# Cross-attention maxima over all 13 tiles and three tiles earlier, shift rows as pieces copied by VectorE

## What is computed

```python
x = x + attend(adaln(x) @ Wq, adaln(ctx) @ Wkv) @ Wp          # "a0": cross-attention, context normalised
x = x + g * (attend(adaln(x) @ qkv) @ Wp)                     # "s1": self-attention
x = x + attend(ln(x) @ Wq, ctx @ Wkv) @ Wp                    # "c1": cross-attention, context raw
x = x + g * mlp(adaln(x))                                     # "m1"
x = x + g * (attend(adaln(x) @ qkv) @ Wp)                     # "s2"
x = x + attend(ln(x) @ Wq, ln(ctx) @ Wkv) @ Wp                # "c2": cross-attention, context normalised
x = x + g * mlp(adaln(x))                                     # "m2"
x = x + gate * experts(x, ctx)                                # "l3"
# attend: softmax(q k^T / sqrt(8)) v for each of the 16 heads
```

## Time and profile before

| what | value |
|---|---|
| time, median of 3 runs | 6270.36 us (6269.71 to 6271.52) |
| the profiled execution | 6276.06 us |
| its span in the profile | 6274.1 us |
| PE busy | 89% of the span |
| DVE busy | 66% |
| ACT busy | 69% |
| POOL busy | 16% |
| the chain that ended last | PE 63%, ACT 14%, DVE 10%, issue 4%, DMA 4%, POOL 3% |

### The profile page before, as it was taken

How to read it: one execution, slowest core, us unless ns; L and a number is a source line. 1 busy time by engine, 2 the same in 40 slices (tenths; PEclk the granted TensorE clock), 3 DMA queues, 4 the chain that set the end, 5 groups by cost and what they waited for, 6 DMA issues and landing times.

```text
span 6274.1 us, 225170 instructions
## 1 busy us (share of the span) xinstructions
PE 5577.9 (89%) x99544; PEld 3439.1 (55%) x99544; DVE 4131.0 (66%) x6523; ACT 4303.3 (69%) x8158; POOL 986.0 (16%) x1660
## 2 busy tenths in 40 slices
PE   5999999989878899999999878699999999998998
PEld 3555555555544455565556444355555555555665
DVE  5777777677555677777777355477777777754443
ACT  3777777777766688788887566467777777763333
POOL 3121121121111111111111011111221211200000
PEclk9999999999999999999999899899999999999999
DMA  2222212222112222222222011222222222211110
GB/s 89 83 67 65 85 57 75 73 61 79 42 57 66 86 74 69 75 86 77 77 67 76 11 59 57 70 61 85 69 63 85 67 65 85 65 52 32 46 57 26
DMA packets 230088, 414.17 MB, mean 66 GB/s; under 512 B 23904, under 2 KB 131472, under 8 KB 228624
## 3 DMA queue, kind: packets, MB, share of 16 engines
q1 hardware_dynamic: 229136, 400.04, 21.3%
HBM read 316.81 MB, written 83.14 MB: 64 GB/s over the span
## 4 chain that ended last, share of the span: by engine, by line
PE 63%; ACT 14%; DVE 10%; issue 4%; DMA 4%; POOL 3%; SPq 2%; DVEq 0%; ACTq 0%; POOLq 0%
PE bank L1087 23%; PE pair L1087 15%; PE bank L1195 12%; ACT P L1329 6%; DVE MX L1493 5%; ACT QP L1340 2%; DMA QP<-scr_q 2%; ACT REST L1300 2%; PE bank L700 2%; PE bank L691 1%; PE pair L627 1%; ACT KSF L1299 1%; PE pair L1182 1%; PE bank L1114 1%; DMA scr_ks<-KSF 1%
## 5 line engine op out<-in xcount | busy, mean ns | idle before, releaser
L1329 ACT ACTIVATE P<-bank 128x512 f32<-128x512 f32 (+1 forms) x5504 | 3185.4, 599 | 1080.0 <-PE bank L1087 1003.5
L1493 DVE TENSOR_REDUCE MX<-pair 128x2 f32<-128x802 f32 x3072 | 2927.6, 987 | 1088.5 <-PE pair L1087 1062.3
L1087 PE MATMUL bank<-QP,KP 128*32 128x256 bf16 (+2 forms) x40192 | 2167.9, 275 | 232.9 <-ACT P L1329 177.5
L1087 PE MATMUL pair<-KP,QP 96*32 96x401 bf16 (+2 forms) x25336 | 1801.3, 337 | 144.9 <-DMA QP<-scr_q 108.4
L1087 PEld LDWEIGHTS bank<-QP,KP 128*32 128x32 bf16 (+2 forms) x40192 | 1057.8, 96 | 1326.5 <-ACT P L1329 292.4
L1195 PE MATMUL bank<-P,VA 128*25 128x256 f32 (+1 forms) x22016 | 1739.1, 384 | 19.1 <-issue 18.6
L1087 PEld LDWEIGHTS pair<-KP,QP 96*32 96x32 bf16 (+1 forms) x25336 | 691.6, 97 | 347.3 <-DVE MX L1493 129.9
L1195 PEld LDWEIGHTS bank<-P,VA 128*25 128x25 f32 (+1 forms) x22016 | 625.7, 104 | 205.7 <-issue 76.9
L1497 DVE TENSOR_REDUCE MX<-pair 128x4 f32<-128x1024 f32 x256 | 311.3, 1222 | 332.3 <-PE pair L1087 331.5
L1618 POOL COPY VA<-VN 128x416 f32<-128x416 f32 (+1 forms) x320 | 140.7, 440 | 2360.8 <-PE bank L1195 2283.9
L1340 ACT CAST QP<-pair 2x512 bf16<-2x512 f32 x640 | 339.4, 576 | 144.1 <-PE pair L1182 132.2
(11 more groups left out here) (242 smaller groups left out, 4189.4 us busy)
## 6 DMA issues: line engine op xcount, KB each, us to landing
KP<-scr_k SPq DMA_DIRECT2D x768, 225.1 KB
QP<-scr_q SPq DMA_DIRECT2D x960, 48.0 KB
CN<-ctx_n SPq DMA_DIRECT2D x40, 768.0 KB
scr_k<-KSF SPq DMA_DIRECT2D x48, 600.8 KB, 3.2
scr_k<-KSF SPq DMA_DIRECT2D x48, 600.0 KB, 3.3
CT<-ctx_t SPq DMA_DIRECT2D x24, 800.5 KB, 4.5
KP<-scr_ks SPq DMA_DIRECT2D x128, 144.0 KB
scr_q<-QS SPq DMA_DIRECT2D x80, 192.0 KB, 2.1
```

What stands on the lines that cost most here:

```text
L1087: last = nc.tensor.matmul(out[c:c + m, :], lhsT[:, c:c + m], rhs, start=start, stop=stop)
L1329: nc.scalar.activation(P[v % 2][0:kt, half * 2 * N:(half + 1) * 2 * N], SC[half][0:kt, :], ACT.Exp, scale=SCALE).then_inc(sem("probs_full" ...
L1493: nc.vector.tensor_reduce(MX[:, r, c:c + 2], MP[j % 2][:, :].rearrange("p (t k) -> p t k", t=2)[:, :, 0:SPANS[0][1]], AX.X, ALU.max).then_ ...
```

## The change

In cross phases: `early` lays the 16 maximum steps evenly over 13 tiles, and `maxima` moves them three tiles ahead (`EARLY = 3`), so that steps 0 to 3 of the group after next run in tiles 10 to 12, and steps 4 to 15 of the next group in tiles 0 to 9. The shifts are then made in tile 9. The shift rows become two pieces of the MISC bank, "r" pieces in tiles 11 and 12 of each group; their products are made by PE and their copies to QP by DVE instead of ACT. The scores of tile 0 wait for those pieces' `misc_free`. In the shifts, the bf16 part is a second reduction of MX instead of a copy of NMF. The pieces of the next element get other slots. d and e are now made in strips of 32 columns. Self phases keep their order, but their last tile adds steps 0 to 3 for a cross phase that follows.

```diff
+EARLY = 3
-SHORT = ["mean", "var", "q", "k0", "k1", "k2", "k3", "y"]
+SHORT = ["mean", "var", "q", "k0", "k1", "k2", "k3", "d", "e", "y"]
...
+    def early(self, first, end):
+        return [j for j in range(self.nm) if first <= j * self.nt // self.nm < end]
+
     def prep_slots(self, host):
         if host.cross:
-            at = dict(mean=0, square=1, var=2, norm=2, q=6, v0=36)
+            at = dict(mean=0, square=1, var=2, norm=2, q=6, v0=34)
             if self.cross:
-                at.update({n: 5 + j * 8 // 13 for j, n in enumerate(STATS)})
-                at.update(ctx_scale=12, ctx_norm=12, t0=18, t1=19, k0=20, k1=22, t2=23, t3=24, k2=26, k3=28)
-                at.update(v1=38, v2=40, v3=45)
+                at.update({n: j * 8 // 13 for j, n in enumerate(STATS)})
+                at.update(ctx_scale=8, ctx_norm=8, t0=14, t1=15, k0=16, k1=18, t2=19, t3=20, k2=21, k3=23)
+                at.update(v1=36, v2=40, v3=42)
...
+            if ph.cross:
+                for g in range(NG if nxt else NG - 1):
+                    pieces += [(g * ph.nt + ph.nt - 2 + half, "rows", "r%d%d" % (g, half)) for half in range(2)]
...
+    def maxima(self, g, t):
+        ahead, far, nt = self.group(g + 1), self.group(g + 2), self.ph.nt
+        if not self.ph.cross or not ahead or not ahead[0].cross:
+            return [(*ahead, j) for j in ahead[0].maximum_at((t, nt))] if ahead else []
+        if t >= nt - EARLY:
+            p = t - (nt - EARLY)
+            return [(*far, j) for j in far[0].early(p, p + 1)] if far and far[0].cross else []
+        return [(*ahead, j) for j in ahead[0].early(t + EARLY, t + EARLY + 1)]
+
+    def maxima_behind(self, g, t):
+        if self.ph.cross or g < NG - 1 or t < self.ph.nt - 1 or not self.nxt or not self.nxt[0].cross:
+            return []
+        return [(*self.nxt, 1, j) for j in self.nxt[0].early(0, EARLY)]
...
 # PE, piece
+                if role == "rows":
+                    ph, b, g = el.group(int(name[1]) + 1)
+                    pe.wait_ge(sem("shift_ready"), ph.c.at("shift_ready", b, g + 1))
+                    for r in range(4):
+                        last = nc.tensor.matmul(MISC[MR:MR + 2, r * 128:(r + 1) * 128],
+                                                NMB[g % 2][:, 4 * int(name[2]) + r, :], IDB[:, :], start=True, stop=True)
+                    last.then_inc(sem("misc_full"), 1)
+                    return
 # PE, scores
                 if t == 0:
-                    pe.wait_ge(sem("rows_done"), at("rows_done", b, 2 * g + half + 1))
+                    use, pair = rows_at[ph.name, b, g]
+                    if use is not None:
+                        pe.wait_ge(sem("misc_free"), use + half + 1)
+                    else:
+                        pe.wait_ge(sem("rows_done"), pair + half + 1)
 # PE, maximum
-                if j >= 2:
-                    pe.wait_ge(sem("max_done"), at("max_done", b, g * ph.nm + j - 1))
+                wait(pe, "max_done", at("max_done", b, g * ph.nm + j - 1))
 # PE, element
-                        js = ahead[0].maximum_at((t, ph.nt)) if ahead else []
+                        js = el.maxima(g, t)
...
-                        if ahead and t == ph.shift_tile:
+                        if ahead and not ph.cross and t == ph.shift_tile:
                             shift_rows(*ahead)
                         for piece_ in behind:
-                            piece(el, *piece_)
+                            piece(el, *piece_, then if piece_[1] in SHORT else 128)
+                        for j in el.maxima_behind(g, t):
+                            maximum(*j)
 # ACT
+                if role == "rows":
+                    return
-                        if ahead and t == ph.shift_tile:
+                        if ahead and not ph.cross and t == ph.shift_tile:
                             copy_rows(*ahead)
 # DVE, piece
+                if role == "rows":
+                    g, half, use = el.group(int(name[1]) + 1)[2], int(name[2]), el.use(role, name)
+                    dve.wait_ge(sem("misc_full"), use + 1)
+                    nc.vector.tensor_copy(QP[g][MR:MR + 2, half * 2 * N:(half + 1) * 2 * N], MISC[MR:MR + 2, :]).then_inc(
+                        sem("misc_free"), 1)
+                    return
 # DVE, shifts
-                dve.wait_ge(sem("shift_step"), at("shift_step", b, 2 * g + 1))
-                nc.vector.tensor_copy(NMB[g % 2][:, :, 0], NMF[:, :]).then_inc(sem("shift_step"), 1)
+                nc.vector.tensor_reduce(NMB[g % 2][:, :, 0], parts, AX.X, ALU.max, negate=True).then_inc(
+                    sem("shift_step"), 1)
```

More of the change, by code:

```diff
@@ L291, in build, with rows_before @@
         ph.misc_after = misc
+    rows_at, pairs = {}, 0
+    for ph in plan:
+        if isinstance(ph, Phase):
+            if ph.el["before"]:
+                rows_at[ph.name, 0, 0] = (None, pairs)
+                pairs += 2
+            for el in [ph.el["first"]] + [ph.el["middle"](i) for i in range(1, B - 1)] + [ph.el["last"]]:
+                for g in range(NG if el.nxt else NG - 1):
+                    t_ph, t_b, t_g = el.group(g + 1)
+                    if ph.cross:
+                        rows_at[t_ph.name, t_b, t_g] = (el.use("rows", "r%d0" % g), None)
+                    else:
+                        rows_at[t_ph.name, t_b, t_g] = (None, pairs)
+                        pairs += 2
+    def rows_before(ph, b, g):
+        if g or b:
+            return rows_at[(ph.name, b, g - 1) if g else (ph.name, b - 1, NG - 1)]
+        return rows_at[ph.before.name, B - 1, NG - 1] if ph.before else None
     stream_total = {k: (ph.misc_after, ph.after().get("stream_done", 0) if not isinstance(ph, LastPhase) else 0)
@@ L1093, in piece @@
                     return
+                use = el.use(role, name)
+                wait(pe, "misc_free", use)
+                if role == "rows":
[6 more added lines that the diff above has]
+                    return
                 ph, b = el.owner(role)
-                at, use = ph.c.at, el.use(role, name)
-                wait(pe, "misc_free", use)
+                at = ph.c.at
                 if name == "mean":
@@ L1157, in maximum @@
                     pe.wait_ge(sem("packed_loaded%d" % g), at("packed_loaded%d" % g, b, ph.c.per["packed_loaded%d" % g]))
-                elif j == 1:
-                    wait(pe, "rows_done", at("rows_done", b, 2 * g))
-                if j >= 2:
-                    pe.wait_ge(sem("max_done"), at("max_done", b, g * ph.nm + j - 1))
+                elif j == 1 and rows_before(ph, b, g) and rows_before(ph, b, g)[1] is not None:
+                    pe.wait_ge(sem("rows_done"), rows_before(ph, b, g)[1] + 2)
+                wait(pe, "max_done", at("max_done", b, g * ph.nm + j - 1))
                 for k in range(2):
@@ L1203, in element @@
                 for g in range(NG):
-                    ahead = (ph, b, g + 1) if g + 1 < NG else (*el.nxt, 0) if el.nxt else None
+                    ahead = el.group(g + 1)
                     for t in range(ph.nt):
-                        js = ahead[0].maximum_at((t, ph.nt)) if ahead else []
+                        js = el.maxima(g, t)
                         third = -(-len(js) // 3)
@@ L1214, in element @@
                         for j in js[:third]:
-                            maximum(*ahead, j, first)
+                            maximum(*j, first)
                         for piece_ in among:
@@ L1240, in _ @@
                         shift_rows(ph, 0, 0)
+                        if ph.cross:
+                            for j in ph.early(0, EARLY):
+                                maximum(ph, 0, 1, j)
                     if ph is plan[0]:
@@ L1515, in element @@
                 for g in range(NG):
-                    ahead = (ph, b, g + 1) if g + 1 < NG else (*el.nxt, 0) if el.nxt else None
                     for t in range(ph.nt):
                         among, behind = el.here(g * ph.nt + t)
-                        mine = ahead[0].maximum_at((t, ph.nt)) if ahead else []
+                        mine = el.maxima(g, t)
                         third = -(-len(mine) // 3)
                         for j in mine[:third]:
-                            maximum(*ahead, j)
+                            maximum(*j)
                         if not ph.cross:
@@ L1526, in element @@
                         for j in mine[third:]:
-                            maximum(*ahead, j)
-                        if mine and mine[-1] == ahead[0].nm - 1:
-                            shifts(*ahead)
+                            maximum(*j)
+                        if mine and mine[-1][3] == mine[-1][0].nm - 1:
+                            shifts(*mine[-1][:3])
                         for piece_ in (among if ph.cross else []) + behind:
                             piece(el, *piece_)
+                        for j in el.maxima_behind(g, t):
+                            maximum(*j)
             for ph in plan:
```

9 lines of the change are left out of this document (6 added, 3 removed).

## The result

The changed kernel takes 6522.06 us (median of 4 runs, 6515.70 to 6524.26), the kernel before, run beside it, 6270.94 us: a ratio of 1.0397, 95% interval 1.0379 to 1.0415. It is slower, as forecast, and for the main reason given, but by 251 us instead of 120, and above the range (6490). The profiled execution took 6515.70 us.

What follows compares the result with a forecast made beforehand. PE and DVE both bind at 1.43 us a tile in tiles 0 to 10, with some 1.2 us lost per group tail. 6276.1 - 168 + 255 + 19 + 14 = 6396, less 5.7: 6390 us; range 6275 to 6490.

Steps and rivals of the forecast that it cites:

- The wait for CN (+255): First groups of a0 and c2: statistics moved to tile 0 wait for CN's load; 29 x 8.8 us lost.
- The clock (+14): Behind each of 29 pauses PE runs at the low clock; 0.5 us each, 14 us (0 to 75).
- That upper end: Low clock binding behind every pause: four microseconds at half speed, two thirds felt; 75 us, total about 6450 us.
- Pieces moved (+19): v0 and v1 leave tiles without maxima and cost PE in full: 0.4 us per element, 47 elements; k2, k3 sum nothing.
- The bare group (-168): Groups outside the 29 first ones: 19.0 us falls to 17.95, gain 1.05 us (0.4 to 1.5) in 160 groups.
- the walk through tiles 10 to 14: Group tail: second row product waits for DVE to free the small bank, after maximum (0.89) and copy (0.6); 0.45 us lost.
- included above: Bare group: DVE's maxima, and through them PE, wait behind the row copies, said to be counted in the 1.05 us gain.
- rival D: Group tail: the rows' wait only changes place, to DVE's copy; gain 0.4 us a group, 6494 us, chance 0.08.
- my lower bound of 0.4: Bare group's smallest gain, in us: tiles with one maximum may run at the 1.21 to 1.3 us their chain needs.
- C: Rival: low clock after each pause lasts and binds, DVE copies cut the group gain to 0.6 us; 6498 us, chance 0.2.
- A: Rival, groups outside the 29: bare group at the products' 16.9 us, rows hidden, gain 2.1 us; 6208 us, chance 0.12.
- B: Rival, first groups: CN lands earlier or DVE's catching up is hidden, 5 us each; 6266 us, chance 0.05.

Runs made afterwards that it cites:

- e5: Changed kernel with 36 dummy products that keep PE busy while it waits for CN in 29 elements; 6494.2 us, 1.0357 of the kernel before.
- e11: Changed kernel with the row products and DVE's row copies at partition 0, the shift rows left out of the computation; 6475.0 us, 1.0329 of the kernel before.
- e3: Changed kernel with the row copies made by ACT, behind both exponentials of the tile; 6517.8 us, 1.0386 of the kernel before.
- e4: Changed kernel with CN loaded earlier and each row copy ahead of its tile's maximum on DVE; 6175.1 us, 0.9839 of the kernel before.
- e12: e4 with the row products and copies at partition 0, the shift rows left out of the computation; 6119.7 us, 0.9756 of the kernel before.

## Why the prediction was right in sign and short in size

**What bounds the kernel, and the tail.** The pace of steady tiles held: the tiles with one maximum run at 1.22 to 1.28 us and those with two at 1.57, as the prices of the earlier trace rows and the lower bound named in the text had it.

**The wait for CN (+255): right.** 29 waits, as forecast; DVE's idle time in them is 244.7 us, 8.4 us each. From the start of the KP loads to DVE's first statistic are 10.9 us (11.1 forecast), and from there to the end of the second row copy 26.3 us, where I added up 24.8. The 1.5 us between hold a wait that I had excluded ("without idling"), 0.88 us for ACT's RSTD, and 0.5 us for the two dearer copies (below). By e5 that wait is the price of the low clock, for which I had 0.5 us in an item of its own. The first groups take 36.6 us in a0 where 35.2 and 0.5 for the clock were forecast. With the clock's item they cost 275 us by the table, and I had 255 + 14 = 269.

**The clock (+14): right in kind, half the size.** 28 us by e5. In the window at 0.50 above PE is busy for 6.1 us behind the pause. The Trainium skill (TensorE: Matmul & The Clock Gate, HAM oscillation) says of a kernel in which TensorE waits for each load that every burst behind a wait starts at the low clock, and the trace agrees: the granted clock was 0.50 around each of the 29 pauses. But the full price, some 6450 us in all, does not follow, since DVE needs 6.1 of the 7.0 us at either clock (e5). That upper end was also added up wrongly: four microseconds at half speed hold two at full speed, so two thirds of their cost are 1.3 us, 39 us in all and not 75, and a total near 6415 us.

**Pieces moved (+19): right in sign, about half the size, and not where I put it.** Second and third group of c1, which hold k2, k3, v0 and v1, together take 43.6 us after and 43.9 before, and two bare groups gain 0.34; so these four cost the same in their new places, v0 and v1 too. The fourth group, with v2 and v3, takes 20.4 for 20.3 where a bare one gains 0.17: some 0.24 us per element, about 11 us over 47 elements.

**The bare group (-168): this step failed.** It was to fall from 19.0 to 17.95 us, and fell from 18.93 to 18.76. By the table, everything but the 29 first groups brings 36 us where the prediction has 168 - 19 = 149; these 113 us and the 6 of the first groups are the whole miss, the 120 us between the profiled execution and 6396. Two terms of the walk through tiles 10 to 14 were wrong:
- The price of a copy among maxima. I took 0.89 + 0.6 = 1.49 us, from a neighbour in the earlier trace rows that works at partition 0; at partition 96 it is 1.75. The row product's wait became 0.76 us instead of 0.45, and at the cheap price it is 0.43 (e11). The price of the nearest row was right for its shape and wrong for its place.
- A wait that the sum does not have. After the second row product comes the second copy, again behind a maximum, and the scores of tile 0's second half wait for it. DVE is then backed up by two copies and a maximum, and tile 12 takes 2.13 us where my prices give 1.97 (1.22, 0.3 for four row products, 0.45 for the wait), and tile 0 takes 1.74 where they give 1.22. I said that those waiting behind the copies were "included above", and checked DVE's sum (16.6 us, "no bound") instead of when each copy ends.

So rival D describes what happened: "the rows' wait only changes its place (scores of tile 0 wait for DVE's copy instead of ACT's)", for the reason named there, a maximum ahead of each copy. I gave it 0.08 and the gain 0.4; the gain was 0.17, below my lower bound of 0.4, which rested on the pace of tiles with one maximum and left out the tail. The range ended at 6490 us, under the times of both slower rivals (C 6498, D 6494), which had 0.28 of the chance between them. Two sums were off as well: the forecast's own bounds give 6275 to 6481 us, not 6300 to 6480, and A and B leave out the clock's 14 us. D's place in the code could be read before: on DVE the maxima of a tile come ahead of its pieces. e3 shows that leaving the copies on ACT would not have helped, and e4 what the change is worth without the wait for CN and the late copy: 18.27 us a group and 6175 us. With the cheap place of the copy as well (e12) a bare group takes 17.77 us, just under the forecast 17.95, and the time is 6120 us, against the 6121 of the forecast without its items for CN and the clock; so the two terms above account for what the tail fell short by, to within a few us.

## What to carry to other kernels

Moving work ahead in a queue moves its wait, too: ask for each moved instruction when its data land, and take the load's issue along; here another place for the load's issue was worth 4%. Let a range take in the rivals that you hold possible. For an engine that shares a small bank with others, the busy sum is not enough: write down when each copy ends, with what stands ahead of it in its queue, and put it ahead of long work that does not need it, provided its producer is a tile ahead. In these runs a price taken from a like instruction held only where it started at the same partitions as its neighbours.

## What was not expected of the hardware

- A DVE copy of 2x512 at partition 96 between reductions at partition 0 costs 1.02 + 0.73 us start to start; the same copy at partition 0 costs 0.90 + 0.60.
- A DVE operation of 512 elements out of PSUM took about as long on two partitions as on 128: 0.67 us for the 2x512 copy at partition 0 (e11), 0.68 for the 128x512 operation of the earlier trace rows.
- The low clock around a pause of PE of 8 to 10 us (granted 0.50 for up to 10.2 us) cost 1.0 us beyond the pause itself, nearly all of it one wait of 0.88 us for ACT, since DVE's own work behind the pause took 6.1 us at either clock.
